# Two wide cross-attention layers: Q tiles of three batches in the first, kept context halves and one engine for both unloadings in the second

## The reference

```python
# first wide layer (L1): RMS norm of x, no rotation, no mask
q = rms_norm(x) @ wq        # [16,100,1024]
k, v = ctx @ wk, ctx @ wv   # [16,361,1024]
x = x + softmax(q k^T) v @ wo
# second wide layer (L2): rotary positions on Q and K, key mask, layer norm after
q, k, v = rope(x @ Wq), rope(ctx @ Wk), ctx @ Wv
x = layer_norm(x + softmax(q k^T / 8, mask) v @ Wo)
```

## Time and profile before

| what | value |
|---|---|
| median of 3 runs | 2019.13 us |
| the profiled execution | 2018.0 us |
| its span, first to last instruction | 2016.1 us |
| mean granted TensorE clock | 0.985 of full |
| first batch of the first wide layer starts at | 472.52 us |
| first scores of the second wide layer at | 1054.43 us |
| O added for the last batch of the second (L1759) | 1682.33 us |

### The profile page before, as it was taken

One profiled execution on the slowest core, in us unless ns is written; L12 is line 12 of the kernel. 1 busy time (PEld: TensorE's weight loads), 2 busy tenths in 40 slices (PEclk: granted clock), 3 DMA queues, 4 the chain that ended last, 5 costly groups with the idle time before them and its releaser, 6 DMA issues. The chain is left out here.

```text
span 2016.1 us, 50639 instructions
## 1 busy us (share of the span) xinstructions
PE 1899.3 (94%) x18654; PEld 1644.1 (82%) x18654; DVE 1443.3 (72%) x3163; ACT 1291.5 (64%) x3129; POOL 598.3 (30%) x740
## 2 busy tenths in 40 slices
PE   7799998999999999999999999999999998898998
PEld 6677777898888888888887887887888877777786
DVE  5688875546555555555589899999999974677775
ACT  4577776556656565566566666666666663777775
POOL 3233230000000000000076677777776730000000
PEclk8899999999999999999999999999999997999999
DMA  5444442201101001000102000000100002443441
GB/s 159 151 148 142 125 134 68 92 25 61 28 21 28 17 22 29 21 24 21 42 25 59 20 20 26 23 23 18 30 22 19 22 14 69 126 128 120 128 134 56
DMA packets 111774, 123.02 MB, mean 61 GB/s; under 512 B 45964, under 2 KB 101420, under 8 KB 111532
## 3 DMA queue, kind: packets, MB, share of 16 engines
q1 hardware_dynamic: 111244, 119.26, 20.0%
q10 hardware_dynamic: 288, 0.51, 0.1%
HBM read 82.29 MB, written 37.45 MB: 59 GB/s over the span
## 5 line engine op out<-in xcount | busy, mean ns | idle before, releaser
L645 ACT ACTIVATE L_P<-PS,MX 100x361 f32<-100x361 f32 x512 | 252.6, 565 | 126.8 <-DVE MX L775 126.8
L775 DVE TENSOR_REDUCE MX<-PS 100x2 f32<-100x722 f32 x256 | 219.9, 901 | 52.9 <-PE PS L525 52.7
L537 PE MATMUL PP<-CON,L_P 100*128 100x100 f32 x1536 | 180.8, 254 | 26.7 <-DVE L_PT L782 22.1
L1544 ACT ACTIVATE wide_V<-PJ 105x512 f32<-105x512 f32 (+1 forms) x143 | 84.1, 594 | 165.5 <-PE PJ L1375 165.5
L1579 ACT ACTIVATE wide_P<-wide_P,MX 100x361 f32<-100x361 f32 x256 | 149.9, 588 | 59.6 <-DVE MX L1717 57.8
L537 PEld LDWEIGHTS PP<-CON,L_P 100*128 100x128 f32 x1536 | 148.5, 142 | 47.4 <-ACT L_P L645 33.9
L1579 ACT ACTIVATE wide_P<-PS,MX 100x361 f32<-100x361 f32 x256 | 140.4, 563 | 70.0 <-DVE MX L1722 70.0
L1442 PEld LDWEIGHTS PS<-CON,wide_P 100*128 100x128 f32 x1536 | 159.6, 140 | 29.4 <-ACT wide_P L1579 8.1
L1442 PE MATMUL PS<-CON,wide_P 100*128 100x100 f32 x1536 | 176.9, 250 | 4.1 <-ACT wide_P L1579 3.1
L1938 POOL TENSOR_TENSOR wide_AC<-wide_T,wide_COSM 128x362 f32<-128x362 f32 x128 | 133.2, 1041 | 155.2 <-issue 155.2
L1455 PEld LDWEIGHTS PP<-wide_PT,wide_V 128*64 128x64 f32 (+1 forms) x3072 | 137.0, 137 | 38.1 <-issue 38.0
(11 more groups left out here) (252 smaller groups left out, 5627.2 us busy)
## 6 DMA issues: line engine op xcount, KB each, us to landing
strips<-L_KS SPq DMA_DIRECT2D x256, 90.5 KB
L_KA<-strips SPq DMA_DIRECT2D x64, 362.0 KB, 3.1
wide_RB<-recip SPq DMA_DIRECT2D x128, 100.0 KB, 2.8
C<-ctx_t SPq DMA_DIRECT2D x32, 361.0 KB, 3.1
kept<-L_CTH SPq DMA_DIRECT2D x16, 361.0 KB, 4.8
kept<-L_CTL SPq DMA_DIRECT2D x16, 361.0 KB, 5.4
L_CTH<-kept SPq DMA_DIRECT2D x16, 361.0 KB, 4.2
L_CTL<-kept SPq DMA_DIRECT2D x16, 361.0 KB, 5.0
```

What stands on the lines that cost most here:

```text
L537: last = nc.tensor.transpose(PPB[:, n, SQ * t:SQ * t + SQ], P[:, (4 * g + 2 * i + n) % 8, 128 * t:128 * t + 128], ident[0:SQ, 0:SQ])
L645: nc.scalar.activation(P[:, (4 * g + j) % 8, 0:SK], PSB[0:SQ, j, 0:SK], ACT.Exp, bias=MX[:, s % 2, 4 * q + j:4 * q + j + 1], scale=1.0).th ...
L775: nc.vector.tensor_reduce(MX[:, s % 2, 4 * q + 2 * i:4 * q + 2 * i + 2], PSB[0:SQ, 2 * i:2 * i + 2, 0:SK], AX.X, ALU.max, negate=True).the ...
L1544: nc.scalar.activation(V[0:r, 1024 * t + 512 * part:1024 * t + 512 * part + 512], bank(key)[0:r, 0:512], ACT.Copy).then_inc(Z["v_taken"], 1)
```

## The change

Three parts, all in `wide_layers`:

- In the first layer query rows are taken in groups, `GROUPS`: batches 0 and 1, 2 and 3, then 4 to 6, 7 to 9, 10 to 12, 13 to 15. A Q product of a group of three has 300 columns. Its eight products stand six in the batch before the group (slots 0 to 3: 1, 2, 2, 1) and two in slots 0 and 1 of the group's first batch. `QH` and `QL` hold the same 2400 columns as before. The second layer keeps pairs; for its first pair all eight Q products stand in batch 15, two to a slot. X is one job for each block of 128 rows. In slots without a `late` job the last V product of `mid` is put behind the second turn.
- The context halves of the first layer are written to memory (`keep`) and read back for the second (`fetch`), where nothing is loaded into `C` or split any more. K products of the second layer wait for the read.
- In the second layer ScalarE unloads the first pair too, behind its `first` jobs and ahead of the other high halves.

```diff
@@ jobs_at
-                if s % 2 == 0 and s + 2 < NS:
+                if s + 1 in GROUPS and s + 1 < B:
+                    late += [("Q", s + 1, p) for p in Q_AHEAD[d]]
+                if s in GROUPS and 0 < s < B:
+                    late += [("Q", s, p) for p in Q_WITHIN.get(d, ())]
+                if s == B - 1:
+                    late += [("Q", B, 2 * d), ("Q", B, 2 * d + 1)]
+                if s >= B and s % 2 == 0 and s + 2 < NS:
                     late.append(("Q", s + 2, 4 + d))
-                if s % 2 and s + 1 < NS:
+                if s > B and s % 2 and s + 1 < NS:
                     late.append(("Q", s + 1, d))
-                if s % 2 and d == 3 and s + 3 < NS:
-                    late.append(("X", s + 3, 0))
+                if d == 3 and s + 2 in GROUPS and s + 2 <= B:
+                    late += [("X", s + 2, k) for k in range(KE)]
+                if d == 3 and s + 3 in GROUPS and s + 3 > B:
+                    late += [("X", s + 3, k) for k in range(KE)]
...
+                if not late and mid and mid[-1][0] == "V":
+                    late.append(mid.pop())
                 return first, mid, late
...
+            GROUPS = {0: 2, 2: 2, 4: 3, 7: 3, 10: 3, 13: 3, **{s0: 2 for s0 in range(B, NS, 2)}}
+            Q_AHEAD, Q_WITHIN = {0: (0,), 1: (1, 2), 2: (3, 4), 3: (5,)}, {0: (6,), 1: (7,)}
@@ SyncE
+                    def keep(s):
+                        sp.wait_ge(Z["c_low"], KE * (s + 1))
+                        for part, half in enumerate((CTH2, CTL2)):
+                            sp.dma_start(halves_dram[s, part], half[:, s % 2, :, 0:SK].bitcast(fp32)).then_inc(kept_out[s % 2], 16)
+
+                    def fetch(s):
+                        sp.wait_ge(Z["made"], job_no["V", s - 2, 5] + 1)
+                        for part, half in enumerate((CTH2, CTL2)):
+                            sp.dma_start(half[:, s % 2, :, 0:SK].bitcast(fp32), halves_dram[s - B, part]).then_inc(s_c[s % 2], 16)
...
-                            if d == 3 and s + 3 < NS:
+                            if d == 3 and s + 3 < B:
                                 context(s + 3)
+                            if d == 0 and 2 <= s + 1 < B:
+                                keep(s + 1)
+                            if d == 2 and B <= s + 2 < NS:
+                                if s < B:
+                                    sp.wait_ge(kept_out[s % 2], 32 * (B // 2))
+                                fetch(s + 2)
@@ TensorE, keys
-                        pe.wait_ge(Z["c_low"], KE * (s + 1))
+                        if rope(s):
+                            pe.wait_ge(s_c[c], FETCHED + 32 * ((s - B) // 2 + 1))
+                        else:
+                            pe.wait_ge(Z["c_low"], KE * (s + 1))
@@ ScalarE
                         act.wait_ge(Z["turned"], 2 * g + 2)
                         if g >= 4:
                             act.wait_ge(Z["weighed"], g - 1)
-                        nc.scalar.activation(PT[:, 2:4, :], PSB[:, 2:4, 0:KV_TILES * SQ], ACT.Copy).then_inc(Z["unloaded_second"], 1)
+                        n = 2 * (g % 2)
+                        nc.scalar.activation(PT[:, n:n + 2, :], PSB[:, n:n + 2, 0:KV_TILES * SQ], ACT.Copy).then_inc(unloaded(g)[0], 1)
...
                             job(key)
+                        if B <= s < NS:
+                            unload(2 * G)
                         for key in turns_of(G - 1)[1:]:
                             rotated_high(key)
-                        if d == 3 and s + 2 < NS:
+                        if d == 3 and s + 2 < B:
                             for k in range(KE):
                                 context_high(s + 2, k)
@@ VectorE
-                        if s < NS:
+                        if s < B:
                             unload(2 * G)
...
-                        if d == 3 and s + 2 < NS:
+                        if d == 3 and s + 2 < B:
                             for k in range(KE):
                                 context_low(s + 2, k)
```

More of the change, by code:

```diff
@@ L70, in build @@
         strips_dram = nc.dram_tensor("strips", (2, 4, 32, 4, SKE), fp32, kind="Internal").ap()
+        halves_dram = nc.dram_tensor("halves", (B, 2, 128, KE, SK), fp32, kind="Internal").ap()
         recip_dram = nc.dram_tensor("recip", (2, H // 2, 128), fp32, kind="Internal").ap()
@@ L1215, in wide_layers @@
             WO_AT = {(0, 1): [0, 1], (B, 3): [2], (B + 1, 0): [3]}
-            Y = XN[:, 0, :]
+            Y = local("Y", [SQ, E])
             def rope(s):
                 return s >= B
+            GROUPS = {0: 2, 2: 2, 4: 3, 7: 3, 10: 3, 13: 3, **{s0: 2 for s0 in range(B, NS, 2)}}
+            STARTS = list(GROUPS)
+            START_OF = {s0 + u: s0 for s0, n in GROUPS.items() for u in range(n)}
+            Q_AHEAD, Q_WITHIN = {0: (0,), 1: (1, 2), 2: (3, 4), 3: (5,)}, {0: (6,), 1: (7,)}
             def jobs_at(s, d):
@@ L1342, in _ @@
                     context(2)
+                    keep(0)
+                    keep(1)
                     for s in range(NS):
@@ L1434, in scores @@
                             for n, r in halves:
-                                last = nc.tensor.matmul(score_bank(g, n)[0:SQ, 0:SKE], Q_[r, q_slot(s, p), q], K_[r, p, :], start=m == 0, stop=m == 2)
+                                last = nc.tensor.matmul(score_bank(g, n)[0:SQ, 0:SKE], q_at(Q_, s, p)[r, q], K_[r, p, :], start=m == 0, stop=m == 2)
                         last.then_inc(Z["scored"], 1)
@@ L1532, in key_or_query @@
                         if not rope(s):
[L1533 removed]
+                            hi, n, done = (KH[:, p, :], SKE, "k_high") if kind == "K" else (q_at(QH, s, p), q_columns(s), "q_high")
+                            plain_high(key, hi, n, done)
                             return
@@ L1800, in _ @@
                     nc.vector.memset(P[:, :, SK:SKP], 0.0).then_inc(Z["padded"], 1)
-                    for v in range(2):
-                        x_stats(0, v)
+                    x_stats(0)
                     x_moments(0)
@@ L1811, in _ @@
                     split_low(2)
-                    for key in FIRST[2:5]:
+                    for key in FIRST[2:6]:
                         job(key)
                     split_low(3)
-                    for key in FIRST[5:8]:
+                    for key in FIRST[6:9]:
                         job(key)
                     split_low(4)
-                    for key in FIRST[8:1 + HP]:
-                        job(key)
-                    for v in range(2):
-                        x_stats(2, v)
-                    x_moments(2)
-                    for key in FIRST[1 + HP:5 + HP]:
+                    for key in FIRST[9:6 + HP]:
                         job(key)
                     split_low(5)
-                    x_norm(2)
-                    for key in FIRST[5 + HP:2 + 2 * HP]:
+                    for key in FIRST[6 + HP:2 + 2 * HP]:
                         job(key)
@@ L1873, in _ @@
                             post_stats(s - 1)
-                        if s % 2 and s + 3 < B:
+                        if s + 2 in GROUPS and s + 2 < B:
                             if d == 1:
-                                for v in range(2):
-                                    x_stats(s + 3, v)
+                                x_stats(s + 2)
                             if d == 2:
-                                x_moments(s + 3)
+                                x_moments(s + 2)
                     post_stats(NS - 1)
@@ L1969, in _ @@
                                 table(s + 2, SINM, sin)
-                        if s % 2 and s + 3 < B and d == 2:
-                            x_rstd(s + 3)
+                        if d == 2 and s + 2 in GROUPS and s + 2 < B:
+                            x_rstd(s + 2)
                         if B < s < NS and d == 2:
```

136 lines of the change are left out of this document (74 added, 62 removed).

## The result

The changed kernel takes 1993.15 us (median of 4 runs, 1990.12 to 1996.91), against 2019.65 us for the kernel before beside it: a ratio of 0.9864, 95% interval 0.9841 to 0.9888. The forecast was 1975 us with a range of 1965 to 1992, so the direction is right, 26.5 us came instead of 44, and the time lies 1.2 us above the range.

The account below looks back on a forecast made before the run. First layer bound by TensorE's stream, second by VectorE's lateness with TensorE close under it. Terms -7.0 - 0.4 - 31.6 - 3.5 - 1.8 = -44.3 us from 2018.0 gave 1973.7, for a median 1975 us; range 1965 to 1992.

Parts of the forecast that it names:

- Q products: First layer: 48 products at 0.74 us become 32 of 300 columns at 0.89; -7.0 us, between -10.9 and -1.0.
- The rival of a cost in proportion: First layer: a 300-column Q product takes 1.11 us, so that layer gains nothing; 1982 us, chance 0.07.
- each one taken out counts in full: First layer: bound by TensorE's stream alone, so each matmul removed saves its whole cost; basis of -7.0 us.
- The X job that the sum took out of the lead-in: Ahead of batch 0: one X job, four transposes and their wait, leaves; -0.4 us (0 to -0.7).
- 0.9 us of stalls: Batches 14 and 15: stalls allowed with four more Q tiles on GpSimd; 73.8 us, -1.8, between -2.7 and +6.
- The GpSimd chain in slot 1 of even batches: Second layer: K copy, two rotations, then a Q low half delay scores; 1.0 us of stall every second batch.
- 0.3 us in hand, ... I take 0: Second layer: ScalarE's second unloading ends in time for the second scores; cost 0, far end +0.68 us a slot.
- Batch 30: End of second layer: 33.4 us of TensorE plus 2.4 of stalls gives 35.8 us instead of 38.80; -3.0.
- The last batch: End of second layer, where little but TensorE's own work is left; -0.5 us.
- half of the stalls stay: Second layer: GpSimd's chain and ScalarE's in-order waits hold the slots, 16 us less gain; 1991 us, chance 0.20.
- nothing would wait for the kept halves' DMA: Both layers: two writes or reads a batch land under cover; 0 on the path, up to 5 us a batch otherwise.
- The other side, slower: Second layer: ScalarE ends each slot, unloading 0.68 us later in 64 slots, 43.5 us; 2054 us, chance 0.03.

Follow-up runs that it names:

- q_joined_late: Changed kernel, but VectorE joins the previous slot's Q tiles after this slot's K shuffles and its unloading, not ahead of them; 1985.59 us, ratio 0.9843 to the kernel before.
- slot2_on_vector: Changed kernel, but in slot 2 of the second layer's batches the first unloading is VectorE's as before; 1997.85 us, ratio 0.9879 to the kernel before.
- q_late_slot2: Changed kernel with Q tiles joined behind the K shuffles and the second layer's slot 2 first unloading on VectorE; 1992.12 us, ratio 0.9871 to the kernel before.
- v_copied_after: q_joined_late, but in slot 2 of the second layer ScalarE does the second unloading ahead of the V product's copy; 1984.67 us, one run.
- all four orders: Changed kernel with Q joined late, output product ahead of chunks, V copied after unloading, awaited Q tile's low half on VectorE; 1980.91 us, ratio 0.9804 to the kernel before.
- pairs_4_to_9: Changed kernel with the first layer's batches 4 to 9 in three pairs instead of two groups of three; 1996.96 us, one run.

## Why the prediction was wrong, point by point

From batch 0 to batch 31 the sum had -43.4 us and -27.5 came. Of the 15.9 us missing, 6.8 are in batches 14 and 15, 6.5 in batches 16 to 29 and 3.4 in batches 0 to 13; batch 30 gave 0.8 more than forecast.

**Q products, right in price, half as much in effect.** The six matmuls of a Q product of 300 columns, from the timeline:

```profile
954.90 0.38 PE L1423 MATMUL PP<-wide_XTH,wide_WH 128*128 128x300 f32 x1
955.12 0.30 PE L1423 MATMUL PP<-wide_XTL,wide_WH 128*128 128x300 f32 x1
...
955.67 0.30 PE L1423 MATMUL PP<-wide_XTH,wide_WL 128*128 128x300 f32 x1
```

0.77 us for five steps and 0.14 for the sixth: 0.91, forecast 0.89. The rival of a cost in proportion (1.11) is out; the formula on the Trainium skill's page "TensorE: Matmul & The Clock Gate" (section "Back-to-back issue gap") gives 128 ns for 300 columns, near the 0.14 measured, and 86 for 200, where the rows have 0.11. A group of three takes 108.02 us, where three batches took 109.4: 1.4 us, forecast 12 x 0.74 - 8 x 0.89 = 1.8. The rest of the error is batch 0, which lost its four Q products (3.0 us) and became only 0.8 us shorter. The step that failed is "each one taken out counts in full". Three things fill the place. The X job that the sum took out of the lead-in (-0.4) was not gone: it stands in slot 3 of batch 0 now and takes 0.4 us there. The exponentials of the second pair come late: with no Q product at the end the last V product stands behind the second turn, the two turns follow each other directly, and the twelve transposes take 1.29 us from start to start (1.41 in slot 2) where two turns take 0.92 in the kernel before; one of their weight loads, at 484.53, waits for ScalarE's last exponential, which ends at 484.39:

```profile
483.50 1.51 PE L1493 MATMUL PS<-CON,wide_P 100*128 100x100 f32 x12
484.79 0.48 PE L1423 MATMUL PP<-wide_WH,wide_CTH 128*128 128x512 f32 x1
```

And the Q product covered VectorE's unloading, which now shows ahead of the scores of slots 1 and 3:

```profile
486.69 0.41 PE L1486 MATMUL PS<-wide_KH,wide_QH 64*100 64x362 f32 x2 [0.26 <-DVE wide_PT L1785]
...
501.68 0.41 PE L1486 MATMUL PS<-wide_KH,wide_QH 64*100 64x362 f32 x2 [0.28 <-DVE wide_PT L1785]
```

"TensorE busy 100%" was read as "nothing else is near". I looked at 687.01 to 759.96, not at batch 0.

**Batch 15: forecast 40.5 us at most likely, up to 46; measured 46.6.** The term "0.9 us of stalls" failed. I had counted GpSimd's load (37.8 of 40 us; measured 33.46) and named the join of the second Q, but put no price on what stands behind that join on VectorE: the shuffles of K, and so the banks. It is an order, not a load and not a shortage of buffers: a fifth buffer left the length as it was, joining Q behind the shuffles took 3.9 us off, 1.7 of them by the clock. Another 1.55 us went in slot 1, where VectorE's 3.2 us of weight chunks stand ahead of the output product's bank; joining Q late leaves 0.47 us of that idle, and swapping the chunks as well leaves none. And behind the idle of 3.18 us the granted clock fell, for which the sum had no term: TensorE was busy 1.7 us longer than in q_joined_late (below). For the two batches the prediction allowed -2.7 to +6, and +5.0 lies in it, but its upper end stood for a Q tile too many in each of the four slots, which is not what happened.

**The second layer's batches: forecast 519.2, measured 525.7.** The GpSimd chain in slot 1 of even batches was right in place, and smaller: 0.6 us instead of 1.0, and the run that takes the tile off GpSimd confirms it. What failed is "0.3 us in hand, ... I take 0". In slot 2, only 7.66 us long, ScalarE waits 1.91 us for VectorE's maxima and then runs without a gap from 1311.22; with both unloadings the second ended at 1317.0, where the second scores could have started at about 1316.7. That, and the V product's bank, make slot 3 9.89 and 10.09 us where the first layer has 9.06 and 9.44: 1.5 us in two batches for which the sum had nothing. The three runs that try to take only this away each move it: to VectorE's shuffle (slot2_on_vector, q_late_slot2) or back into slot 1 (v_copied_after). What is left in slot 3 after all four orders, some 0.4 to 0.5 us, stays open.

**Batch 30: forecast -3.0, measured -3.8, partly by luck.** The prediction took its length over TensorE's own 33.4 us for VectorE's lateness. But 2.4 of the 3.8 us are TensorE's busy time, 36.29 us before at a granted clock of 0.96 and 33.91 after at 1.00. The last batch, for which the sum had -0.5, became 0.8 us longer; why stays open.

**The gain by part.** In batches 16 to 29 14.0 us need the kept halves, 5.9 need the unloading, and 5.2 come by either. The rival "half of the stalls stay" (1991 us, chance 0.20) lies nearest to the time measured, but not for its reason: in the second layer 25.1 of 40.2 us of stalls went, where it had 16. That the sum ends near it is the chance meeting of the errors of 6.8, 6.5 and 3.4 us listed above. That nothing would wait for the kept halves' DMA was right: no wait for one appears in the two layers, and batches 0 to 14 are as long without the writes.

**The other side, slower,** did not come: ScalarE's lateness costs about 0.5 us a batch, at one slot of four, not 0.68 at each.

## What to carry to other kernels

Taking load off the busiest engine pays until a chain of short steps over four engines sets the slot; from there look, for each wait in an in-order queue, at what stands behind it that could go ahead. When tiles per slot double on such a chain, price the loop (here shuffle, copy, rotation, join, next shuffle) against the shortest slot, not the engine's load against the batch. An engine that is 100% busy can still be covering a wait of others: read the stretch from which work is taken away, not a typical one.

## What the runs showed of the hardware

TensorE's granted clock falls behind some of these stalls, in batches 15 and 16, which were at full clock in the kernel before. In the changed kernel the idle of 3.18 us ahead of 1056.87 is followed by a stretch at a lower granted clock. The stretch 1057 to 1062 of the changed kernel, then slot 0 of batch 16 in q_joined_late and in v_copied_after, which do the same work (columns as in the earlier trace rows, the third number from the end is the granted clock):

```profile
1057.00:1062.00 5.00, 5.00 (x26) 4.42 (x26) 3.91 (x8) 3.94 (x9) 4.05 (x4) 0.66 0.01 1
```

```profile
1054.22:1063.27 9.05, 9.05 (x79) 7.86 (x79) 7.51 (x21) 7.29 (x21) 7.93 (x11) 1.00 0.46 117
```

```profile
1053.86:1065.53 11.67, 11.67 (x79) 10.10 (x79) 7.46 (x21) 7.25 (x20) 8.56 (x12) 0.75 0.36 91
```

A mean of 0.75 is part of the slot at 1.2 GHz, the rest at 2.4, and costs 2.6 us in one slot, as much as all of TensorE's idle in the batch 15 before it. It is why batch 16 takes 36.4 us in one run and 39.0 in another with the same code there, and why batches 17 to 29 are the fairer comparison. An idle time does not decide it alone: in these two runs the longest idle of batch 15 is the same, 1.60 and 1.59 us, and in pairs_4_to_9 an idle of 2.78 us in slot 3 of batch 15 was followed by a full clock to the end of the slot, while slot 2, behind an idle of 1.55 us, had 0.83.

VectorE's low half of K took 1055 ns before and 750 ns after, on the same shapes, though nothing of it was changed. That it now starts at other points of GpSimd's rotations, behind a wait for ScalarE's high half, is the likely reason; no run isolates it. The groups by form of batches 16 to 29 after; the wait that came in its place is 56.4 us:

```profile
L1741 DVE TENSOR_TENSOR wide_KL<-wide_AC,wide_KH 128x362 fp32r<-128x362 f32 x112 | 84.0, 750 | 56.4 <-ACT wide_KH L1579 56.4
```

With the unloading back on VectorE it is 1035 ns again, without that wait. This is also why VectorE's busy time fell below the forecast: 16 such steps in two batches at 0.3 us less are 4.9 us. The Trainium skill, page "SBUF — State Buffer", section "Who interferes with whom", says that a VectorE instruction with two inputs in SBUF contends with a GpSimd instruction that reads SBUF, and that this contention is an exclusive lock. These numbers, and the 514 against 1044 ns of the earlier trace rows, agree with it.
